# The recurrent stage of a decoder kernel: two channel tiles to one scan, and PSUM banks dealt out anew

## What is computed

```
def _selective_scan(u, dt, A, Bm, Cm, Dp):
    dA = jnp.exp(dt[..., None] * A)
    dBu = (dt * u)[..., None] * Bm[:, :, None, :]
    def step(h, inp):
        dA_t, dBu_t, C_t = inp
        h = dA_t * h + dBu_t
        y = jnp.einsum('ben,bn->be', h, C_t)
        return (h, y)
    ...
    return y + u * Dp

def _mamba(x, in_w, cw, cb, xw, dtw, dtb, A_log, Dp, ow):
    xz = x @ in_w
    u, z = jnp.split(xz, 2, axis=-1)
    conv = cb + sum((up[:, k:k + L, :] * cw[:, k] for k in range(K)))
    u = jax.nn.silu(conv)
    dbl = u @ xw
    dt = jax.nn.softplus(dbl[..., :DT_RANK] @ dtw + dtb)
    Bm = dbl[..., DT_RANK:DT_RANK + D_STATE]
    Cm = dbl[..., DT_RANK + D_STATE:]
    y = _selective_scan(u, dt, A, Bm, Cm, Dp)
    return (y * jax.nn.silu(z)) @ ow
```

## Time and profile before

| | |
|---|---|
| median of 3 runs | 4912.89 us (4897.6 to 4913.54) |
| the profiled execution, its own time | 4911.87 us |
| its span, first to last instruction | 4910.2 us |
| mean granted TensorE clock, as a share of 2.4 GHz | 0.919 |
| busy over the span: PE, DVE, ACT, POOL | 83%, 68%, 41%, 46% |
| first and last scan begin at | 83.9 and 2136.1 us |

### The profile page before, as it was taken

How to read it: one execution, slowest core, us unless ns; L and a number is a source line. 1 busy time by engine, 2 the same in 40 slices (tenths; PEclk the granted TensorE clock), 3 DMA queues, 4 the chain that set the end, 5 groups by cost and what they waited for, 6 DMA issues and landing times. The chain is left out here.

```text
span 4910.2 us, 51107 instructions
## 1 busy us (share of the span) xinstructions
PE 4080.8 (83%) x16288; PEld 2279.1 (46%) x16288; DVE 3346.0 (68%) x5430; ACT 2004.3 (41%) x3243; POOL 2258.9 (46%) x1887
## 2 busy tenths in 40 slices
PE   5888888888888888849747887999968999888898
PEld 1233333333333333324422326888833444677798
DVE  4999999999999999974476655444445554144433
ACT  4666666656565666522223451111112444222100
POOL 6888888888888888920020112344330111000320
PEclk7999999999999999979977998999978999877899
DMA  2122221222222222210033311000052320000000
GB/s 78 60 65 79 65 73 63 66 77 72 66 67 76 71 65 67 72 44 0 0 96 41 46 19 50 20 27 26 1 152 53 52 44 10 15 10 0 26 18 30
DMA packets 223223, 240.91 MB, mean 49 GB/s; under 512 B 100481, under 2 KB 131516, under 8 KB 222716
## 3 DMA queue, kind: packets, MB, share of 16 engines
q1 hardware_dynamic: 222972, 237.82, 18.1%
HBM read 209.58 MB, written 25.69 MB: 48 GB/s over the span
## 5 line engine op out<-in xcount | busy, mean ns | idle before, releaser
L473 POOL TENSOR_TENSOR arena<-arena 128x512 f32<-128x512 f32 x1024 | 1279.5, 1270 | 290.1 <-DVE arena L760 283.0
L760 DVE TENSOR_TENSOR_SCAN arena<-psum,arena 128x512 f32<-128x512 f32 x1024 | 1274.6, 1245 | 91.9 <-POOL arena L473 51.5
L865 PE MATMUL psum<-arena,base 128*128 128x512 f32 x2048 | 1113.6, 645 | 263.2 <-DVE arena L735 258.5
L638 ACT ACTIVATE psum<-arena 128x512 f32<-128x512 f32 x1024 | 704.4, 689 | 773.5 <-DVE arena L760 770.2
L865 PEld LDWEIGHTS psum<-arena,base 128*128 128x128 f32 x2048 | 358.5, 196 | 902.0 <-DVE arena L735 743.9
L224 POOL TENSOR_TENSOR rounded<-arena,rounded 128x512 fp32r<-128x512 f32 (+2 forms) x181 | 315.5, 1749 | 835.0 <-DVE rounded L220 835.0
L735 DVE TENSOR_TENSOR arena<-arena,psum 128x512 f32<-128x512 f32 x1024 | 677.1, 661 | 0.3 <-PE psum L838 0.3
L230 PE MATMUL psum<-rounded 128*128 128x256 f32 (+1 forms) x1728 | 561.8, 325 | 37.1 <-DVE arena L1650 16.4
L231 PE MATMUL psum<-rounded 128*128 128x256 f32 (+1 forms) x1728 | 561.1, 325 | 2.0 <-issue 2.0
L232 PE MATMUL psum<-rounded 128*128 128x256 f32 (+1 forms) x1728 | 560.4, 324 | 0.0
L1119 DVE TENSOR_REDUCE arena<-psum 128x1 f32<-128x512 f32 (+3 forms) x768 | 403.2, 554 | 191.6 <-PE psum L1182 129.9
(11 more groups left out here) (278 smaller groups left out, 5480.0 us busy)
## 6 DMA issues: line engine op xcount, KB each, us to landing
arena<-mb_b_rows SPq DMA_DIRECT2D x512, 256.0 KB, 3.1
arena<-L_ffn_w SPq DMA_DIRECT2D x34, 512.0 KB, 4.3
arena<-f_parts SPq DMA_DIRECT2D x96, 128.0 KB, 7.2
arena<-l_parts SPq DMA_DIRECT2D x96, 128.0 KB, 6.7
l_v<-arena SPq DMA_DIRECT2D x16, 512.0 KB, 3.9
arena<-l_v SPq DMA_DIRECT2D x32, 256.0 KB, 4.3
f_parts<-arena SPq DMA_DIRECT2D x24, 256.0 KB, 2.4
l_parts<-arena SPq DMA_DIRECT2D x24, 256.0 KB, 2.3
```

Source lines behind the costliest of these rows:

```text
L473: eng.tensor_tensor(drive[:, u % RD, :], dtu[:, g % 2, m, :], b_sb[:, v % RB, :], ALU.mult)\
L638: eng.activation(ps[:, DECAY + u % 2, :], dt[:, g % 2, m, :], ACT.Exp, scale=a_neg[:, g // 4 % 2, m, n:n + 1]).then_inc(decay_ready, 1)
L760: eng.tensor_tensor_scan(h[:, u % RH, :], ps[:, DECAY + u % 2, :], drive[:, u % RD, :], first, ALU.mult, ALU.add).then_inc(scanned, 1)
L865: mm = eng.matmul(ps[:, Y + u % 2, :], sh.ident, hc[:, u % RW, :], start=False, stop=n == NS - 1)
```

## The change

A unit becomes a **pair**: both channel tiles that share a state. A segment has 32 pairs j (`of_pair`), in the order of the units before.

- One scan runs over 1024 elements: two tiles of `drive` and two PSUM banks of decay (four banks, two pairs in turn) lie end to end. The second tile must not go on from the first: ACT writes its decay from element 1 on, and element 0 of that bank is 0.0 for good. In odd segments the second tile's carry is added into the first element of its drive on POOL (`carry_in`, with `first_decay` on ACT).
- One product with C and one `drive` cover 1024 elements, with the rows of C and B broadcast over the two tiles; `gate` covers two tiles.
- C has one bank in place of two, and `spread` of the next pair comes first in PE's iteration. The front has one bank in place of two (four in the first segment's front, which runs alone).
- The steps of the front get new places, and so do some of their waits. `exponential` now has four ACT instructions (Exp, add 1, Ln, subtract 1), and `remainder` one on POOL where it had two. `copy_z` 1 to 3, `gate_z` and `exponential` 2 and 3 move into the next segment. `out_projection` is cut in two halves.
- The rings hold 4 pairs of `drive`, 3 of h and 2 of hc. `rem`, the tile of `remainder`, exists once for each m.

The diff, cut to its core:

```diff
-    Y, C_BANK, DECAY, FRONT = 0, 2, 4, 6
+    Y, C_BANK, FRONT, DECAY = 0, 2, 3, 4
...
-        return ps[:, FRONT + k % 2, :]
+        return ps[:, DECAY + k % 4 if k < STEPS else FRONT, :]
 
     def wait_taken(eng, k):
-        eng.wait_ge(taken[k % 2], k // 2 + 1)
+        eng.wait_ge(taken, k + 1)
 
     def wait_bank_free(eng, k):
-        if k >= 2:
-            eng.wait_ge(taken[k % 2], k // 2)
+        if k >= STEPS:
+            eng.wait_ge(taken, k)
+        elif k >= 4:
+            eng.wait_ge(taken, k - 3)
...
-            eng.wait_ge(exped, f * M + m + 1)
-            eng.tensor_scalar(rem, ey[:, m, :], 1.0, 1.0, ALU.add, ALU.subtract).then_inc(soft, 1)
-            eng.wait_ge(soft, n + 1)
-            eng.tensor_tensor(rem, ey[:, m, :], rem, ALU.subtract).then_inc(soft, 1)
+            eng.wait_ge(logged, f * M + m + 1)
+            eng.tensor_tensor(rem[:, m, :], ey[:, m, :], rem[:, m, :], ALU.subtract).then_inc(soft, 1)
...
+        def carry_in(v):
+            g, half, n = of_pair(v)
+            m = 2 * half + 1
+            if n == 0:
+                eng.wait_ge(step0_ready, g // 2 * 2 + half + 1)
+                eng.wait_ge(carried, carries((g - 1) * PAIRS + half * HALF + HALF - 1))
+                eng.tensor_tensor(inject[:, half, :], step0[:, half, :], carry[:, :, m], ALU.mult).then_inc(injected, 1)
+                eng.wait_ge(injected, g // 2 * 2 + half + 1)
+            first = drive[:, v % RD, 1, 0:1]
+            eng.wait_ge(drive_ready, drives(v) - 1)
+            eng.tensor_tensor(first, first, inject[:, half, n:n + 1], ALU.add).then_inc(drive_ready, 1)
...
-            eng.tensor_tensor(drive[:, u % RD, :], dtu[:, g % 2, m, :], b_sb[:, v % RB, :], ALU.mult)\
-                .then_inc(drive_ready, 1)
+            eng.tensor_tensor(drive[:, v % RD], dtu[:, g % 2, 2 * half:2 * half + 2, :],
+                              b_sb[:, v % RB, :].unsqueeze(1).to_broadcast([P, 2, BANK]), ALU.mult).then_inc(drive_ready, 1)
+            if g % 2:
+                carry_in(v)
...
+                if j == 7:
                     remainder(g, 2)
-                elif p == 10:
+                elif j == 8:
                     logarithm(g, 2)
-                elif p == 12:
+                elif j == 9:
                     dt_times_u(g, 2)
-                elif p == 14:
+                elif j == 12:
                     remainder(g, 3)
-                elif p == 16:
+                elif j == 13:
                     logarithm(g, 3)
-                elif p == 18:
+                elif j == 14:
                     dt_times_u(g, 3)
...
+                elif j == 29:
                     remainder(f, 0)
-                elif p == 56:
+                elif j == 30:
                     logarithm(f, 0)
-                elif p == 57:
                     dt_times_u(f, 0)
-                elif p == 58:
+                elif j == 31:
                     remainder(f, 1)
-                elif p == 60:
                     logarithm(f, 1)
-                elif p == 61:
                     dt_times_u(f, 1)
...
-            eng.activation(log_y[:, m, :], ey[:, m, :], ACT.Ln, bias=1.0).then_inc(logged, 1)
+            eng.wait_ge(exped, (f * M + m) * 2 + 1)
+            eng.activation(rem[:, m, :], ey[:, m, :], ACT.Identity, bias=1.0).then_inc(exped, 1)
+            eng.activation(log_y[:, m, :], ey[:, m, :], ACT.Ln, bias=1.0)
+            eng.wait_ge(exped, (f * M + m) * 2 + 2)
+            eng.activation(rem[:, m, :], rem[:, m, :], ACT.Identity, bias=minus).then_inc(logged, 1)
...
+            if v >= 2:
+                eng.wait_ge(scanned, v - 1)
+                before_g, before_half, before_n = of_pair(v - 2)
+                if before_g % 2 == 0:
+                    eng.activation(carry[:, before_n, 2 * before_half:2 * before_half + 2], h[:, (v - 2) % RH, :, BANK - 1], ACT.Copy)\
+                        .then_inc(carried, 1)
...
+            for k in range(2):
+                m = 2 * half + k
+                eng.activation(ps[:, DECAY + 2 * (v % 2) + k, k:], dt[:, g % 2, m, k:], ACT.Exp,
+                               scale=a_neg[:, g // 4 % 2, m, n:n + 1]).then_inc(decay_ready, 1)
+            if g > 0:
+                if j < 3:
+                    copy_z(g, j + 1)
+                elif j == 3:
+                    gate_z(g)
+                elif j == 5:
+                    exponential(g, 2)
+                elif j == 10:
+                    exponential(g, 3)
...
+                if j == 4:
                     deviation(f)
-                elif 9 <= p < 13:
-                    normalize(f, p - 9)
-                elif p == 14:
-                    rows(f, 0)
-                elif p == 16:
-                    rows(f, 1)
-                elif p in (21, 23, 25, 27):
-                    tap(f, (p - 21) // 2)
-                elif p == 28:
+                elif j in (6, 7):
+                    normalize(f, 2 * (j - 6))
+                    normalize(f, 2 * (j - 6) + 1)
+                elif j in (8, 9):
+                    rows(f, j - 8)
...
+                elif j in (11, 13, 15, 17):
+                    tap(f, (j - 11) // 2)
+                elif j == 16:
                     gate_u(f, 0)
-                elif p == 32:
+                elif j == 19:
                     gate_u(f, 1)
-                elif p == 34:
+                elif j == 20:
                     next_head(f)
-                elif p == 36 and f % 4 == 0:
+                elif j == 21 and f % 4 == 0:
                     decays_of(f // 4)
-                elif p == 40:
+                elif j == 25:
                     rows_of_x(f)
-                elif p == 41:
                     high_rows(f)
-                elif p in (44, 46, 48, 50):
-                    step(f, (p - 44) // 2)
-                    if p == 46:
-                        mid_rows(f)
-                elif p in (45, 47, 49, 51):
-                    exponential(f, (p - 45) // 2)
-                elif p == 52:
+                if j in (27, 28, 29, 30):
+                    step(f, j - 27)
+                if j == 27:
+                    mid_rows(f)
+                elif j == 28:
+                    exponential(f, 0)
+                elif j == 29:
                     low_rows(f)
-                elif p in (53, 55, 57, 59):
-                    copy_z(f, (p - 53) // 2)
-                elif p == 60:
-                    gate_z(f)
+                elif j == 30:
+                    exponential(f, 1)
+                elif j == 31:
+                    copy_z(f, 0)
...
+            eng.tensor_tensor(hc[:, v % RW], h[:, v % RH], ps[:, C_BANK, :].unsqueeze(1).to_broadcast([P, 2, BANK]), ALU.mult)\
+                .then_inc(weighted, 1)
...
+            first = 0.0 if g % 2 == 0 else carry[:, n, 2 * half:2 * half + 1]
+            slot = DECAY + 2 * (v % 2)
+            eng.tensor_tensor_scan(h[:, v % RH].rearrange("p q s -> p (q s)"), ps[:, slot:slot + 2, :].rearrange("p q s -> p (q s)"),
+                                   drive[:, v % RD].rearrange("p q s -> p (q s)"), first, ALU.mult, ALU.add).then_inc(scanned, 1)
+            if v > HALF and n == 1:
+                gate((v - 2) // PAIRS, (v - 2) % PAIRS // HALF)
+            if v:
+                weigh(v - 1)
...
+                elif j in (10, 12, 14, 16):
+                    convolve(f, (j - 10) // 2)
+            if g > 0 and j in (20, 22):
+                add_out(g - 1, (j - 20) // 2)
...
+            eng.wait_ge(weighted, v + 1)
+            if v + 1 < ALL:
+                spread(v + 1)
             if n == 0:
-                skip_path(g, m // 2, m % 2)
-            eng.wait_ge(weighted, u + 1)
-            mm = eng.matmul(ps[:, Y + u % 2, :], sh.ident, hc[:, u % RW, :], start=False, stop=n == NS - 1)
-            if n == NS - 1:
-                mm.then_inc(summed, 1)
-            if p % 2 and u // 2 + 2 < SEGS * (UNITS // 2):
-                spread(u // 2 + 2)
+                skip_path(g, half)
+            for k in range(2):
+                mm = eng.matmul(ps[:, Y + k, :], sh.ident, hc[:, v % RW, k, :], start=False, stop=n == NS - 1)
+                if n == NS - 1:
+                    mm.then_inc(summed, 1)
             if f < SEGS:
-                if p in (10, 12):
-                    turn(f, (p - 10) // 2)
-                elif p in (15, 17, 19, 21):
-                    in_projection(f, 0, (p - 15) // 2)
-                elif p == 33:
+                if j in (5, 6):
+                    turn(f, j - 5)
+                elif j in (8, 10, 12, 14):
+                    in_projection(f, 0, (j - 8) // 2)
+                elif j == 22:
                     x_projection(f)
-                elif p in (39, 41, 43, 45):
-                    dt_projection(f, (p - 39) // 2)
-                elif p in (47, 49, 51, 53):
-                    in_projection(f, 1, (p - 47) // 2)
-            if g > 0 and p in (23, 27):
-                out_projection(g - 1, (p - 23) // 4)
```

(67 more changed lines are left out.)

201 lines of the change are left out of this document (91 added, 110 removed).

## The result

The changed kernel takes **5355.8 us** (median of four, 5352.6 to 5369.8) where the kernel before took 4906.4 beside it: a ratio of 1.092 [1.090, 1.094]. The forecast was slower, at 5202 within 5010 to 5330; the sign and, but for one wait, the places of the loss are as it said, and the size is 154 us too small, just outside the range and on the price of its third rival (5356).

A forecast was written before the change was run, and what follows sets the result against it. DVE's queue was taken to set the pace. From 4911.9 us, -72 for merging, -30 of old waits, +342 of new waits and +50 for PE's clock gave 5202 us, range 5010 to 5330.

The forecast's parts named there:

- third rival: PE falls to half clock in every gap that DVE's waits leave: 5356 us in all; chance 0.14.
- DVE's saving, -72: Merged scans and `weigh`s save fixed instruction time on DVE, 0.108 or 0.173 us a pair: -72 us.
- Convolution, 7.6 a segment: DVE waits 1.9 us before each of four `convolve`s for PE's front product and ACT's `tap`: 7.6 us.
- `add_out`, 5.3: DVE waits for the two halves of `out_projection`, 1.0 us before the first addition and 4.3 before the second.
- x and the turn, 9.9: Scans wait for decays behind `x_projection`, 1.9 us, and at the segment's turn for ACT's decays and POOL's drives, 8.0.
- old waits: Of DVE's 39 us of waits before the change, 30 given back: those behind table loads of `gate_u` and `gate_z`.
- PE's clock: +50, a quarter of 204: PE's clock falls after idle gaps, costing 0 to 204 us; a quarter taken, +50 us.
- 342: DVE's new waits at convolution, `add_out`, x and the turn: 22.8 us for each of 15 segments, +342 us.
- eight new gaps a segment: Waits at convolution, `add_out` and the turn leave PE idle 3 to 5 us, eight times, each losing up to 1.7.
- The first rival: The front keeps ahead, every front product there when DVE asks: faster, 4801 us; chance 0.05.

The follow-up runs named there:

- e8: e7 with each merged scan and each `weigh` cut into two of 512 again; 4863.7 us, 0.991 of the kernel before.
- e3: Changed kernel with 18 products of zeros added on PE in each of three gaps a segment, no step moved; 5257.2 us, 1.073 of the kernel before.
- e1: Changed kernel with `tap`, the convolution and the first gate of u one place later; 5092.9 us, 1.040 of the kernel before.
- e2: Changed kernel with both `add_out` additions one place later, convolution left as it was; 5213.7 us, 1.065 of the kernel before.
- e4: Changed kernel with the moves of e1 and e2 together and `rows_of_x` one place later; 4940.8 us, 1.008 of the kernel before.
- e7: e4 with the x chain earlier, the second half of `out_projection` later, and ACT's and POOL's turn work spread over more places; 4813.7 us, 0.980 of the kernel before.

## Why the prediction came out short

- **DVE's saving, -72: right.** The pairs gain 0.11 and 0.16 to 0.17 us, and DVE's busy time in the stage fell by 68. Its split was partly wrong: of the 0.128 taken as a scan's fixed part in odd segments, e8 gives 0.06 to the carried start.
- The Trainium skill (Perfetto Trace Analysis, Optimizing Scalar/DVE Operations) gives about 125 ns of access overhead for an instruction of DVE on PSUM, by which the estimate was 128 us; the 59 us that e8's timeline shows are under half of that, and the measurement decides. The half throughput of the scan that the Trainium skill states (DVE: opcode table, instruction layouts, handler registers and perf-mode slots, Datapath and trigger behaviour) agrees with the rows: 2.20 us for a scan of 1024, 1.11 for a product.
- **Convolution, 7.6 a segment: right at full clock** (7.3 to 7.5 in e3, where PE's three gaps are filled). As the kernel stands it is 222/15 = 14.8.
- **`add_out`, 5.3: right at full clock too** (0.85 + 4.22 = 5.1 in the segment of e1 shown). As the kernel stands it is 2.2 + 5.9 = 8.1. The places are right: e2 takes the waits away.
- **x and the turn, 9.9: nearly right**, 179.4/15 = 12.0 with 0.5 of old waits behind `gate_z` in it. x is 1.7 (forecast 1.9). In the turn the decay of pair 29 makes 3.0 (1.4, and 1.0 two pairs later that did not come), and POOL's drives 31 and 32 make 2.3 and 4.6 (1.2 and 4.4): the engines are those of the forecast, whatever the row names. POOL's part is hardly PE's clock: it is 102 us in e4 as well, where the stage was granted 0.97. How much of ACT's part is, no run has told apart. Nor was the turn's wait the price of a chain alone: with no operation shortened, e7's spreading brought the scans' waits to 16 us.
- **`weigh` waiting for `spread`, 43 us: not in the list.** It is small where PE has no long gaps (1.0 in e7).
- **The step that failed is PE's clock: +50, a quarter of 204.** By the forecast's own numbers DVE's idle time in the stage would be 44.9 - 30 + 342 = 357 us with PE at full clock; it is 573, 216 more: 108 before `convolve`, 43 before `add_out`, 43 before `weigh` and 22 before the scans. The runs put the first three, 194 us, down to the gaps. e3 takes 112 off the convolution with PE kept at work and no place moved. e1 shows `add_out`'s two waits at the forecast's length where the clock is 1.00. And `weigh`'s waits go as the gaps go: those of pair 24 (28 us) in e2, those of pairs 18 and 19 (14 us) in e1, where pair 24's grow by 5. The other 22 are in part POOL's and stay open. The price of one gap was a little low (1.7 taken, 2.2 measured) and their number a little high (194/15/2.2 = 5.9 where eight were taken); together they were nearly right. The quarter was wrong: it was drawn from the stage's mean clock of before, 0.96, which says how rarely such gaps stood there, and nothing of what each new one costs. The forecast had itself listed eight new gaps a segment, longer than the one it had measured; for these its upper bound was the value. The third rival, at 0.14, held just that.
- That the third rival's 5356 is the measured median to the microsecond is luck. DVE's idle time grew by 12 us more than it holds and DVE saved 4 less, while 15 us fell away outside the stage, where the forecast had put nothing: 4 ahead of it and 11 in the stages behind. Those are not touched by the change and take 2757 to 2774 us in the traces of the ten kernels.
- **The first rival** (the front keeps ahead, 4801) lost in this kernel, and e7, at 4814, comes near its price: PE's idle share was enough, and only the places stood against it.

## What to carry to other kernels

When units of a hand-written order are merged, a place becomes twice as long, and each engine's lead, counted in places, must be worked out anew: put a consumer behind the chain's length, and on an engine that runs ahead put an operation some places behind its producer's (here two or three, with a lead of four). Price a new wait together with what it does to the engine that it leaves idle; if that engine's clock falls in gaps and the engine sits in the chain of the next wait, take the full price of every gap and not an average over a stage that had few. When a wait has several possible causes, find out when each of them ended before believing the one name in the row. A slower result does not condemn the idea: cut the merged operation in two again in the best order (e8) and the merging shows its own worth.

## What was not expected of the hardware

- One wait lengthened the next: 1.82 us the first time, 4.04 to 4.44 the next three, with the same instructions and the same gap of 5.13 us on PE between them, behind which the granted clock was 0.52; 54 added products a segment, which do nothing, saved 99 us.
- A scan of 512 that starts from a value in a tile took 0.06 us longer to the next start than one in the same place that starts from a constant (1.19 against 1.13, the first scan of an odd and of an even pair in e8).
- `drive` of 1024 took 2.35 us on POOL, by the shorter rows (2.43) and not by the one row of that length, 2.92.
